# Queries and keys of layer 1 as two fp16 pieces on half of the array's rows, instead of three bf16 pieces on all of them

## What is computed

```python
def _L1_conv_ref(x, w_qkv, w_proj):
    heads, d, n = 4, 16, h * w
    qkv = jnp.einsum('oc,bchw->bohw', w_qkv, x)
    q, k, v = jnp.split(qkv.reshape(b, 3 * c, n), 3, axis=1)
    attn = jax.nn.softmax(jnp.einsum('bhdn,bhdm->bhnm', q, k) * scale, axis=-1)
    out = jnp.einsum('bhnm,bhdm->bhdn', attn, v).reshape(b, c, h, w)
    return jnp.einsum('oc,bchw->bohw', w_proj, out) + x
```

## Time and profile before

| What | us |
|---|---|
| median of 3 runs | 8849.96 (8849.55 to 8853.73) |
| span of the profiled execution | 8846.4 |
| PE busy | 8390.2 |
| DVE busy | 7476.4 |
| ACT busy | 6313.8 |
| POOL busy | 835.7 |

### The profile page before, as it was taken

How to read it: one execution, slowest core, us unless ns; L and a number is a source line. 1 busy time by engine, 2 the same in 40 slices (tenths; PEclk the granted TensorE clock), 3 DMA queues, 4 the chain that set the end, 5 groups by cost and what they waited for, 6 DMA issues and landing times.

```text
span 8846.4 us, 325856 instructions
## 1 busy us (share of the span) xinstructions
PE 8390.2 (95%) x145926; PEld 4001.2 (45%) x145926; DVE 7476.4 (85%) x9622; ACT 6313.8 (71%) x13874; POOL 835.7 (9%) x676
## 2 busy tenths in 40 slices
PE   4799999999999999999999999999999999999997
PEld 2344444444444444444444444444444444444443
DVE  3789888888888888888888888888888898888885
ACT  1378677776777777677776777777777776777776
POOL 3110101001010010101101010010100101010000
PEclk9799999999999999999999999999999999999998
DMA  1201102020110201102011110201102011020110
GB/s 32 40 14 26 27 18 38 12 38 18 28 27 15 40 15 26 27 13 42 13 26 27 24 33 11 43 16 26 26 15 41 14 26 27 14 42 13 31 20 19
DMA packets 122887, 222.36 MB, mean 25 GB/s; under 512 B 57218, under 2 KB 89090, under 8 KB 121354
## 3 DMA queue, kind: packets, MB, share of 16 engines
q1 hardware_dynamic: 121490, 201.52, 12.5%
HBM read 67.50 MB, written 42.73 MB: 12 GB/s over the span
## 4 chain that ended last, share of the span: by engine, by line
PE 75%; DVE 15%; DMA 4%; SPq 3%; issue 1%; ACT 1%; POOL 0%; POOLq 0%; DVEq 0%; ACTq 0%
PE PS L1248 22%; PE PS L1107 20%; PE PS L1260 19%; DVE small L888 10%; PE PS L1148 3%; PE PS L1168 3%; DVE small L927 1%; PE PS L1200 1%; DMA scratch_att<-o_st 1%; DMA tok_unit<-in_query_ident 1%; PE PS L1138 1%; PE PS L1209 1%; DVE win_scores L930 1%; DMA small<-scratch_att 1%; PE PS L1157 1%
## 5 line engine op out<-in xcount | busy, mean ns | idle before, releaser
L826 ACT ACTIVATE exps<-PS 128x392 f32<-128x392 f32 x12800 | 5488.8, 499 | 2028.4 <-PE PS L1248 1587.7
L888 DVE TENSOR_REDUCE small<-PS 128x1 f32<-128x784 f32 x6400 | 5868.8, 967 | 586.2 <-PE PS L1107 553.1
L1107 PE MATMUL PS<-k_stack,q_stack 96*32 96x392 bf16 x51200 | 3197.9, 334 | 204.4 <-DVE small L888 152.6
L1248 PE MATMUL PS<-q_stack,k_stack 99*32 99x392 bf16 x51200 | 3334.9, 332 | 20.8 <-ACT exps L826 12.7
L1260 PE MATMUL PS<-exps,v_all 128*32 128x392 f32 x25600 | 2665.7, 495 | 0.2 <-ACT exps L826 0.2
L1248 PEld LDWEIGHTS PS<-q_stack,k_stack 99*32 99x32 bf16 x51200 | 1316.3, 95 | 1762.5 <-ACT exps L826 975.1
L1107 PEld LDWEIGHTS PS<-k_stack,q_stack 96*32 96x32 bf16 x51200 | 1182.7, 96 | 1785.3 <-DVE small L888 1092.7
L1260 PEld LDWEIGHTS PS<-exps,v_all 128*32 128x32 f32 x25600 | 760.6, 110 | 355.0 <-ACT exps L826 50.3
L726 POOL TENSOR_TENSOR win_scores<-win_scores,small 128x784 f32<-128x784 f32 x256 | 384.2, 1502 | 1836.5 <-DVE small L939 1836.5
L927 DVE TENSOR_REDUCE small<-PS 128x16 f32<-128x784 f32 x256 | 247.6, 967 | 190.0 <-PE PS L1148 190.0
L1148 PE MATMUL PS<-kmask,tok_unit 113*64 113x392 f32 (+1 forms) x2048 | 376.3, 503 | 18.4 <-DMA tok_unit<-in_query_ident 17.7
(11 more groups left out here) (113 smaller groups left out, 3057.8 us busy)
## 6 DMA issues: line engine op xcount, KB each, us to landing
q_stack<-tok_qk SPq DMA_DIRECT2D x320, 98.0 KB, 3.8
k_stack<-tok_qk SPq DMA_DIRECT2D x320, 98.0 KB, 4.2
kmask<-tok_unit SPq DMA_DIRECT2D x1024, 12.2 KB
att<-scratch_att SPq DMA_DIRECT2D x68, 196.0 KB
z_half<-scratch_z SPq DMA_DIRECT2D x34, 392.0 KB, 7.1
inv_sums<-scratch_rden SPq DMA_DIRECT2D x272, 49.0 KB, 2.1
scratch_att<-o_st SPq DMA_DIRECT2D x512, 26.0 KB
out<-inv_sums SPq DMA_DIRECT2D x68, 196.0 KB, 3.2
```

Of the source, the lines that this page charges most:

```text
L826: nc.scalar.activation(exps(u), PS[:, u % SCORE_BANKS, 0:GTOK], ACT.Exp, scale=D1 ** -0.5).then_inc(s_exps, 1)
L888: nc.vector.tensor_reduce(max_parts[:, n_:n_ + 1], slot(), op=ALU.max, axis=AX.XY)\
L1107: last = mm(PS[32 * r:32 * r + 32, it.bank + j, 0:GTOK], q_stack[0:STACK, stage // 2, q0:q0 + 32], k_stack[0:STACK, stage // 2, chunk * GT ...
L1248: last = mm(PS[32 * r:32 * r + 32, u % SCORE_BANKS, 0:GTOK], k_stack[0:STACK + SHIFT, h, k0:k0 + 32], q_stack[0:STACK + SHIFT, h, c * GTOK ...
```

## The change

Queries and keys are split into two fp16 pieces. Three blocks of 16 rows (high x high, low x high, high x low) make 48 rows, and with two rows for the negated maximum 50. That is under 64, so the stacks stand twice on the partitions, from row 0 and from row 64, and matmuls alternate between the copies: the two chunks of a `max` go to the two halves of the array's rows, issued in turn, and scores use row half `j % 2`, so consecutive scores use different halves. To keep the fp16 pieces in range, `w_qk1` is multiplied by a power of two that is found once, in the setup, from bounds of the weights; the exponential's scale becomes a register. The second piece is made by DVE straight from PSUM; a third copy (the high piece divided by 32) is made by POOL, and `piece_m` is gone. There are still 12 stack DMAs per head; a shift takes four DMAs instead of three. `shift_pieces` has three instructions instead of six. Setup gains 14 small steps on DVE, one matmul on PE and one more fill on POOL.

```diff
-PIECES = 6
+PIECES = 3
 STACK = PIECES * D1
-SHIFT = 3
+SHIFT = 2
...
-        step(at("piece_m", i), at("gqk", i))
-        step(at("piece_l", i), at("piece_m", i))
+        step(at("piece_s", i), (at("gqk", i), 1))
...
-                    for dst, base, order in ((q_stack, 0, (0, 0, 1, 1, 0, 2)), (k_stack, CH, (0, 1, 0, 1, 2, 0))):
+                    for dst, base, order in ((q_stack, 0, (0, 2, 1)), (k_stack, CH, (0, 1, 2))):
                         for j, pc in enumerate(order):
-                            sp.dma_start(dst[D1 * j:D1 * j + D1, h, 0:TOKENS],
-                                         pieces[pc][base + D1 * h:base + D1 * h + D1, :]).then_inc(s_stacks[h], 16)
+                            for s in range(2):
+                                sp.dma_start(dst[CH * s + D1 * j:CH * s + D1 * j + D1, h, 0:TOKENS],
+                                             pieces[pc][base + D1 * h:base + D1 * h + D1, :])\
+                                  .then_inc(s_stacks[h], 16)
...
-                    for pc in range(3):
-                        sp.dma_start(q_stack[STACK + pc:STACK + pc + 1, it.i // 2, t0 * 128:t1 * 128]
-                                     .rearrange("p (t n) -> p t n", n=128),
-                                     neg_rows[(t1 - t0) * pc:(t1 - t0) * (pc + 1), :]).then_inc(s_shift_loaded, 16)
+                    for pc in range(SHIFT):
+                        for s in range(2):
+                            row = CH * s + STACK + pc
+                            sp.dma_start(q_stack[row:row + 1, it.i // 2, t0 * 128:t1 * 128]
+                                         .rearrange("p (t n) -> p t n", n=128),
+                                         neg_rows[(t1 - t0) * pc:(t1 - t0) * (pc + 1), :])\
+                              .then_inc(s_shift_loaded, 16)
...
-            nc.gpsimd.memset(k_stack[STACK:STACK + SHIFT, :, 0:TOKENS], 1.0).then_inc(s_zeroed, 1)
+            nc.gpsimd.memset(k_stack[32:CH, :, 0:TOKENS], UNIT).then_inc(s_zeroed, 1)
             pl.wait_ge(s_zeroed, 10)
+            nc.gpsimd.memset(k_stack[96:128, :, 0:TOKENS], UNIT).then_inc(s_zeroed, 1)
+            pl.wait_ge(s_zeroed, 11)
...
-                    pl.wait_ge(s_piece_m, t * 4 + i + 1)
-                    nc.gpsimd.tensor_tensor(both_sides(pieces[2], i), both_sides(tok_h, i), both_sides(pieces[1], i),
-                                            ALU.subtract).then_inc(s_piece_l, 1)
+                    pl.wait_ge(s_piece_h, t * 4 + i + 1)
+                    nc.gpsimd.tensor_scalar(both_sides(pieces[2], i), both_sides(pieces[0], i), 1 / LOW, 1.0,
+                                            ALU.mult, ALU.mult).then_inc(s_piece_s, 1)
...
-                elif it.kind == "piece_m":
-                    act.wait_ge(s_rest, t * 4 + it.i + 1)
-                    nc.scalar.activation(both_sides(pieces[1], it.i), both_sides(tok_h, it.i), ACT.Copy).then_inc(s_piece_m, 1)
...
                 nc.scalar.activation(exps(u), PS[:, u % SCORE_BANKS, 0:GTOK], ACT.Exp,
-                                     scale=D1 ** -0.5).then_inc(s_exps, 1)
+                                     scale=score_scale).then_inc(s_exps, 1)
...
                 elif it.kind == "gqk":
                     dve.wait_ge(s_piece_h, t * 4 + it.i + 1)
-                    nc.vector.tensor_tensor(both_sides(tok_h, it.i), slot(), both_sides(pieces[0], it.i), ALU.subtract)\
-                      .then_inc(s_rest, 1)
+                    nc.vector.scalar_tensor_tensor(out=both_sides(pieces[1], it.i), in0=both_sides(pieces[0], it.i),
+                                                   scalar=-LOW, in1=slot(), op0=ALU.mult, op1=ALU.add)\
+                      .then_inc(s_piece_l, 1)
...
-                part(nc.vector.tensor_copy(neg_pieces[:, 0:nt], neg_max[:, t0:t1]))
-                part(nc.vector.tensor_tensor(neg_rest[:, t0:t1], neg_max[:, t0:t1], neg_pieces[:, 0:nt], ALU.subtract))
-                part(nc.vector.tensor_copy(neg_pieces[:, nt:2 * nt], neg_rest[:, t0:t1]))
-                part(nc.vector.tensor_tensor(neg_rest[:, t0:t1], neg_rest[:, t0:t1], neg_pieces[:, nt:2 * nt],
-                                             ALU.subtract))
-                nc.vector.tensor_copy(neg_pieces[:, 2 * nt:3 * nt], neg_rest[:, t0:t1]).then_inc(s_max_pieces, 1)
+                part(nc.vector.tensor_scalar(neg_pieces[:, 0:nt], neg_max[:, t0:t1], 1 / UNIT, None, ALU.mult))
+                nc.vector.scalar_tensor_tensor(out=neg_pieces[:, nt:2 * nt], in0=neg_max[:, t0:t1], scalar=1 / UNIT,
+                                               in1=neg_pieces[:, 0:nt], op0=ALU.mult, op1=ALU.subtract)\
+                  .then_inc(s_max_pieces, 1)
...
-                    for j in range(2):
-                        chunk = 2 * pair_ + j
-                        for r in range(4):
-                            q0 = tile * 128 + 32 * r
+                    for r in range(4):
+                        for j in range(2):
+                            chunk, q0 = 2 * pair_ + j, tile * 128 + 32 * r
                             last = mm(PS[32 * r:32 * r + 32, it.bank + j, 0:GTOK],
-                                      q_stack[0:STACK, stage // 2, q0:q0 + 32],
-                                      k_stack[0:STACK, stage // 2, chunk * GTOK:(chunk + 1) * GTOK],
+                                      q_stack[CH * j:CH * j + STACK, stage // 2, q0:q0 + 32],
+                                      k_stack[CH * j:CH * j + STACK, stage // 2, chunk * GTOK:(chunk + 1) * GTOK],
                                       start=True, stop=True)
...
+                rows = slice(CH * (j % 2), CH * (j % 2) + STACK + SHIFT)
...
-                    last = mm(PS[32 * r:32 * r + 32, u % SCORE_BANKS, 0:GTOK], k_stack[0:STACK + SHIFT, h, k0:k0 + 32],
-                              q_stack[0:STACK + SHIFT, h, c * GTOK:(c + 1) * GTOK], start=True, stop=True)
+                    last = mm(PS[32 * r:32 * r + 32, u % SCORE_BANKS, 0:GTOK],
+                              k_stack[rows, h, k0:k0 + 32], q_stack[rows, h, c * GTOK:(c + 1) * GTOK],
+                              start=True, stop=True)
```

More of the change, by code:

```diff
@@ L4 @@
 from collections import namedtuple
+import math
 IMAGES, CH, RES, WIN = 16, 64, 56, 7
@@ L54 @@
     "gqk": (("PE", 660), ("ACT", 720), ("DVE", 890)),
-    "piece_m": (("ACT", 750),), "piece_l": (("POOL", 1600),), "gv": (("PE", 890), ("DVE", 700)),
+    "piece_s": (("POOL", 1000),), "gv": (("PE", 890), ("DVE", 700)),
     "stack": (("SP", 9000),), "vcopy": (("POOL", 470),),
@@ L423, in attention_mlp_kernel @@
             "h_ready", "mlp_in", "mlp1", "hidden", "mlp2", "residual2", "z_ready", "z_mid", "z_stored"))
-        s_gqk, s_piece_h, s_rest, s_piece_m, s_piece_l, s_gv, s_v_staged, s_v_copied = (sem(n) for n in (
-            "gqk", "piece_h", "rest", "piece_m", "piece_l", "gv", "v_staged", "v_copied"))
+        s_gqk, s_piece_h, s_piece_l, s_piece_s, s_gv, s_v_staged, s_v_copied = (sem(n) for n in (
+            "gqk", "piece_h", "piece_l", "piece_s", "gv", "v_staged", "v_copied"))
         s_stacks = [sem(f"stacks_loaded{h}") for h in range(H1)]
@@ new lines, in rebase, with then @@
+            def rebase():
+                def then(ins):
+                    ins.then_inc(s_ranges, 1)
+                    done[0] += 1
+                    dve.wait_ge(s_ranges, done[0])
+                done = [6]
+                top, bits, power = ranges[:, 2:4], ranges[:, 2:4].bitcast(i32), ranges[:, 4:6]
+                dve.wait_ge(s_bounds, 1)
+                then(nc.vector.tensor_reduce(top, PS[:, 7, 128:256].rearrange("p (a c) -> p a c", a=2), op=ALU.max,
+                                             axis=AX.X))
+                then(nc.vector.tensor_scalar(top, top, 2.0 ** -60, None, ALU.max))
+                then(nc.vector.tensor_scalar(bits, bits, 0x7F800000, None, ALU.bitwise_and))
+                then(nc.vector.reciprocal(power, top))
+                for a in range(2):
+                    then(nc.vector.tensor_scalar(w_qk1[:, CH * a:CH * a + CH], w_qk1[:, CH * a:CH * a + CH],
+                                                 power[:, a:a + 1], TOP * LOW, ALU.mult, ALU.mult))
+                then(nc.vector.tensor_tensor(exp_scale, top[:, 0:1], top[:, 1:2], ALU.mult))
+                then(nc.vector.tensor_scalar(exp_scale, exp_scale, D1 ** -0.5 / TOP ** 2, None, ALU.mult))
@@ L848, in _ @@
+            z_limits()
             for r in range(2):
```

80 lines of the change are left out of this document (54 added, 26 removed).

## The result

The changed kernel takes 9127.49 us, the median of four runs (9122.68 to 9137.07), beside 8849.75 of the kernel before on the same chip. The ratio is 1.0314, its 95% interval 1.0299 to 1.0328: 3.1% slower, where 7.6% faster was forecast and the range ended at 8640.

A forecast was written before the change was run, and what follows sets the result against it. DVE was taken to bound the changed kernel at 493 us an image. From 8846.4, 15 x 41.8 and 42 for the last image came off and 1 for setup was added: 8178, as a median 8182, rounded to 8180; range 7930 to 8640.

The forecast's parts named there:

- The step on the halves: PE's maxima and scores: row halves run side by side, taking 66 and 47 us, together 113, off each image.
- the rival in which they don't: PE's row halves do not overlap at the 16-bit pace; 576 us per image, 9500 in all; chance 0.08.
- SP, POOL and DMA ... No cost: Queues of SP, POOL and DMA: one more DMA per shift, 8 per image, is covered by existing waits and costs nothing.
- the four rivals: DVE kept fed (0.06), dear changes of shape (0.08), the order doesn't fit (0.10), halves don't overlap at the 16-bit pace (0.08).
- DVE is the bound ... I take 0.935: Per image DVE needs 461 us, PE 417, ACT 391; DVE busy for 0.935 of the time gives 493, 42 less.
- The order doesn't fit: Same needs of the engines, but waits grow under PE's fixed order: 518 to 534 us an image, 8580 to 8830; chance 0.10.
- The sign that was named for the waits: If right, PE's waits for the reduction (line 888) go up and DVE's waits for `max` (line 1107) go down.
- PE is then occupied for only 0.85: Reason given for taking DVE's busy share as 0.935, nearer to the best stretch (0.957) than to today's mean (0.872).
- the change of shape: PE switching between 64-row work and 128-row weighs: 379 more places per image at 0.10 us, 38 us added.
- Dear changes of shape: Each change on PE costs 0.25 us, so PE needs 474 an image; 515 an image, 8500 in all; chance 0.08.
- the 417: PE's new need per image in us: groups 151, weighs 132, the rest 96, changes 38; in place of 492.
- The clock ... I expect no loss from it: PE's granted clock: no loss expected; under 0.97 in an image's windows would make the prediction wrong.

The follow-up runs named there:

- e2_one_half: Against e1_shift_first, all maxima and scores use row half 0 only, changes of shape kept; 10431.04 us, four runs from 10181.71 to 10631.81.
- e6_half_both: Against e1_shift_first, reductions read only the first of two chunks and exponentials do 196 of 392 columns; 8082.05 us, one run.
- e1_shift_first: The changed kernel with one entry of SP's order moved, the stage 6 shift issued ahead of the stack loads; 8858.6 us, ratio 1.0005 to the kernel before.
- e7_reordered: The changed kernel with PE's letters reordered by a search, its planner told of halves and change costs; 8640.44 us, ratio 0.9756 to the kernel before.

## Why the prediction was wrong

**Right.** The step on the halves: they overlap at the 16-bit pace, a `max` takes one group's time, and the rival in which they don't is out (at the kernel's full clock `e2_one_half` would need 566 an image, near that rival's 576). DVE's floor of 461 (460.8 measured), the price of a reduction (0.916, under the bound of 0.92), the setup (+1; the first score starts 0.5 earlier). That rows alone make a change of shape. An exponential takes 0.502, just over the 0.50 that was named as a sign; it was 0.499 before, and 3 ns more for each of 800 are 2 us an image at most.

**Failed: "SP, POOL and DMA ... No cost".** The step looked at one DMA more per shift and at what stands behind a shift, and took the queue's order as given. But the queue is made by the planner from a table that the change edits, and its new order puts the shift behind 24 issues. That is 220 us of waiting (15 of 14.7), and 269 by the experiment. It is nearly the whole distance between 8850 and 9127, and a bit over a quarter of the 945 between 8182 and 9127. None of the four rivals had it. It could have been worked out from the diff: the cost table is code.

**Failed: "DVE is the bound ... I take 0.935".** With the queue mended an image takes 534.7, not 493. DVE's share is 0.861, not 0.935, under even today's 0.872. This is the rival *The order doesn't fit* (518 to 534), just past its slow end, and it was given 0.10. Its mechanism is shown twice: relief of one engine brings about 200 us and relief of both 777, and another order brings 218 us without less work. The sign that was named for the waits split: PE waits more for the reduction (1093 to 1567), as forecast, but DVE's waits for `max` rose too (553 to 601, and 864 in the kernel after) where they were to fall. The argument "PE is then occupied for only 0.85" took three engines one at a time. Under one fixed order, each `max` that waits for DVE holds up the scores that ACT needs, each score that waits for ACT holds up DVE's next `max`, and a run of weighs and maxima leaves ACT without work. Still open are the 28.7 us an image between the best order tried (521.7) and 493: whether a better order exists was not shown. The last image went the same way: 365 was forecast, with ACT busy for 0.915 of it; it took 419.8, and ACT was busy for 334.6 of them, 0.80 (418.1 with the queue mended, 402.2 with the new order, 407.9 before).

**Mis-sized: the change of shape.** Priced at 0.10, measured 0.11 on the way to a weigh and 0.14 behind it, its own two passes included, 0.25 a weigh: as an estimate, 379 x 0.124 = 47 an image in place of 38. The direction and the kind were right. The Trainium skill says under Key Properties in TensorEngine Tiling (Array Packing) that a change of tiling mode drains the engine; the trace agrees in that each change costs time, 0.11 at full clock where only the rows change, and adds this price. *Dear changes of shape* (0.25 each) did not happen, but this term alone eats 47 of the 113 that the halves were to give back. PE's whole need was not seen in any run: in `e6_half_both`, where DVE and ACT hold back least, an image takes 487, so it is under that; the 417 is neither shown nor refuted.

**Failed: "The clock ... I expect no loss from it".** The image's mean clock is 0.97, just at the bound that the prediction named, and that of the span 0.956 (before 0.983). The stretch it rested on had no stop in it. The change brought a new stop, and the lower level around the old one, at an image's start, mostly lasts longer. What this costs is small beside the other two. At the shift it is at most the 49 us by which the mended queue gave back more than the wait; with the queue mended, it is some 2 us an image: 0.17, the estimate from the images, for each of the 17.8 - 6.3 us more at the lower level.

In sum, an estimate by differences of the image, from 493 to 552.5: 17.8 are the queue (with what the clock did there), 13.0 the order as far as a new one mended it, 28.7 the rest, with the 9 of dearer changes and what the clock costs somewhere in the last two.

## What to carry to other kernels

Where queues are made from a cost table, an edit of the table is an edit of the queues: compare each engine's order before and after, DMA issues first, before pricing anything else. When three engines share one fixed order, the floor of the busiest one says little; ask at each stretch which of the others idles while PE waits, and expect that a faster engine may pay only after the order is made again for the new durations (here 0.9756 in place of 1.0005). If an experiment removes a wait, look for what is late next before believing in its price.

## What was not expected of the hardware

The halves add next to nothing to each other's time: eight matmuls of a `max`, with tails, last 0.36, and the next group starts 0.18 after them. After a stop of about 5 us at an image's start the clock is at its lower level for 20.5 us in nine of fourteen images of the kernel with halves (`e1_shift_first`; 17.1 in one, 6.8 in four), and for 3.4 to 6.8 us in those of the kernel with full rows. And a long stop isn't needed for it. In `e2_one_half` it fell for 112.6 us with PE busy throughout, after 7.9 us with PE busy for 7.8. In `e7_reordered`, with a single stop over 3 us between its second and its last image, an image has 25.8 us of it on average, in stretches of up to 34.1:

```profile
2439.40:2446.40 7.00, 5.72 (x116) 1.81 (x116) 6.82 (x9) 4.38 (x12) 0.52 (x1) 1.00 0.04 9
2446.40:2480.50 34.10, 33.62 (x398) 7.59 (x392) 22.50 (x26) 15.10 (x36) 3.00 (x5) 0.50 0.56 112
```

Which property of the work holds the clock down no run here separates.
